# Six units of lag for the downs and three for the gate products, with tile 1's projection in a bank of its own

## The reference

```python
xw = einsum('ntd,dh->nth', x, Wx) + b
def step(prev_h, xw_t):
    next_h = tanh(xw_t + prev_h @ Wh)          # 32 steps, one after another
xf  = hs                                        # what follows is per token
xn  = xf * rsqrt(mean(xf * xf) + EPS) * norm_scale
logits = xn @ wg + bg
vals, idx = top_k(logits, 4);  gates = softmax(vals)
gate_full = einsum('tke,tk->te', one_hot(idx, 16), gates)
h = einsum('th,ehd->etd', xn, w1) + b1
a = minimum(h[..., ::2], 7.0);  b = clip(h[..., 1::2], -7.0, 7.0)
s = a * sigmoid(1.702 * a) * (b + 1.0)
y = einsum('eti,eih->eth', s, w2) + b2
out = x + hs + einsum('eth,te->th', y, gate_full)
```

## Time and profile before

| | us |
|---|---|
| three timed runs, median (lowest, highest) | 108.16 (108.02, 108.65) |
| the profiled execution, its own time | 107.47 |
| span of its trace | 105.7 |
| TensorE busy | 98.3 (93% of the span) |
| VectorE busy | 67.2 (64%) |
| GpSimd busy | 64.7 (61%) |
| ScalarE busy | 61.7 (58%) |

### The profile page before, as it was taken

One profiled execution on the slowest core, in us unless ns is written; L12 is line 12 of the kernel. 1 busy time (PEld: TensorE's weight loads), 2 busy tenths in 40 slices (PEclk: granted clock), 3 DMA queues, 4 the chain that ended last, 5 costly groups with the idle time before them and its releaser, 6 DMA issues.

```text
span 105.7 us, 1704 instructions
## 1 busy us (share of the span) xinstructions
PE 98.3 (93%) x549; PEld 83.6 (79%) x549; DVE 67.2 (64%) x179; ACT 61.7 (58%) x143; POOL 64.7 (61%) x77
## 2 busy tenths in 40 slices
PE   7778899989999999999999979999999999999980
PEld 2557789978999999999999958888777777777660
DVE  0302357976827996589787997668566556666740
ACT  3354836999755586667736646666555666655400
POOL 6004447997890995639963799689544566544400
PEclk9999999999999999999999999999999999999999
DMA  2999920007930000895048911995100000000003
GB/s 66 224 378 338 374 92 0 0 9 254 398 147 3 0 6 6 212 372 212 5 141 228 366 67 20 274 364 207 34 6 0 3 0 0 0 0 0 0 0 99
DMA packets 5000, 12.97 MB, mean 123 GB/s; under 512 B 752, under 2 KB 1792, under 8 KB 4992
## 3 DMA queue, kind: packets, MB, share of 16 engines
q1 hardware_dynamic: 4672, 12.69, 35.5%
q10 hardware_dynamic: 320, 0.18, 0.6%
HBM read 12.28 MB, written 0.59 MB: 122 GB/s over the span
## 4 chain that ended last, share of the span: by engine, by line
PE 82%; ACT 7%; DMA 2%; DVE 2%; POOL 2%; issue 2%; POOLq 0%; DVEq 0%; ACTq 0%
PE psA L806 20%; PE psB L806 19%; PE psY L836 12%; PE psR L836 7%; PE psR L753 5%; PE psY L753 3%; PE psM L836 3%; PE psR L848 2%; DMA wx_x_sb<-in_wx_x 2%; PE psR L745 2%; PE psM L760 2%; ACT small_h L450 2%; ACT psA L494 2%; PE psM L767 1%; ACT psA L503 1%
## 5 line engine op out<-in xcount | busy, mean ns | idle before, releaser
L414 POOL TENSOR_TENSOR actg<-act,gate_cols 128x512 f32<-128x512 f32 x31 | 39.4, 1281 | 12.5 <-DVE act L713 10.7
L696 DVE TENSOR_SCALAR lin<-psB,one_b1b 128x256 f32<-128x256 f32 (+1 forms) x48 | 26.0, 568 | 18.8 <-PE psB L806 18.8
L494 ACT ACTIVATE psA<-psA,lim_b1a 128x256 f32<-128x256 f32 (+1 forms) x48 | 23.8, 513 | 23.2 <-PE psA L806 23.1
L713 DVE SCALAR_TENSOR_TENSOR act<-lin,psA 128x512 f32<-128x512 f32 x32 | 22.0, 686 | 1.8 <-ACT psA L503 0.6
L503 ACT ACTIVATE psA<-psA,limit_col 128x512 f32<-128x512 f32 x32 | 21.1, 659 | 0.8
L806 PE MATMUL psA<-xn_hi,w_hi 128*128 128x256 f32 (+1 forms) x48 | 18.9, 394 | 0.2
L836 PE MATMUL psY<-actg,w_sb 128*128 128x256 f32 x64 | 17.2, 391 | 0.8 <-POOL actg L414 0.8
L806 PE MATMUL psB<-xn_hi,w_hi 128*128 128x256 f32 (+1 forms) x48 | 16.0, 333 | 0.0
L806 PE MATMUL psB<-xn_lo,w_hi 128*128 128x256 f32 (+1 forms) x48 | 15.6, 324 | 0.0
L806 PE MATMUL psB<-xn_hi,w_lo 128*128 128x256 f32 (+1 forms) x48 | 15.5, 323 | 0.0
L806 PE MATMUL psA<-xn_hi,w_lo 128*128 128x256 f32 (+1 forms) x48 | 15.5, 323 | 0.0
(11 more groups left out here) (87 smaller groups left out, 133.7 us busy)
## 6 DMA issues: line engine op xcount, KB each, us to landing
gate_cols<-gate_rows SPq DMA_DIRECT2D x16, 512.0 KB, 5.7
w_sb<-in_w SPq DMA_DIRECT2D x4, 512.0 KB, 7.3
w_sb<-in_w SPq DMA_DIRECT2D x4, 256.0 KB, 8.3
wx_x_sb<-in_wx_x SPq DMA_DIRECT2D x1, 320.0 KB, 5.9
wx_x_sb<-in_wx_x SPq DMA_DIRECT2D x2, 128.0 KB, 2.7
out<-yT SPq DMA_DIRECT2D x2, 128.0 KB, 4.3
out<-yT SPq DMA_DIRECT2D x1, 192.0 KB, 1.9
small_h<-in_small ACTq DMA_DIRECT2D x1, 105.0 KB, 2.8
```

What stands on the lines that cost most here:

```text
L414: nc.gpsimd.tensor_tensor(by_pair(actg[:, u % SUM_DEPTH, w]), by_pair(act[:, u % ACT_DEPTH, w]), gate_block(u, w), ALU.mult).then_inc(actg ...
L494: last = nc.scalar.activation(psA[u % 2][:, o], psA[u % 2][:, o], ACT.Relu, scale=-1.0, bias=lim_b1a[:, e0 + k:e0 + k + 1])
L696: last = nc.vector.tensor_scalar(lin[:, v % 2, o], psB[v % 2][:, o], one_b1b[:, e0 + k:e0 + k + 1], LIMIT + 1.0, ALU.add, ALU.min)
L713: nc.vector.scalar_tensor_tensor(act[:, v % ACT_DEPTH, 0:w], lin[:, v % 2, 0:w], 1.0 - LIMIT, psA[v % 2][:, 0:w], ALU.max, ALU.mult).then_ ...
```

## The change

`LAG` goes from 4 to 6, `POOL_LAG` from 2 to 3, and the rings grow to 8 and 6 buffers. Since add_h(c) stands in slot UNIT0[c + 1] + LAG, it moves from slot 12 to slot 14 for chunk 0, and from 20 to 22 for chunk 1. In the head, tile 1 is projected into `psX`, its sums go to `psX` too (with semaphores of their own), and tiles 2 to 6 are projected one by one in the head; only tile 7's projection is left in the loop, in slot 10 (before: tiles 5 to 7 at once, in slot 6). Both tiles' raw logits are made together behind the sums of tile 1. ScalarE makes all high parts of w1 ahead of slot 0 (before: six of the 16 calls in slots 0 to 2). The gates of pair 0 are transposed between a(1) and b(1), and copied ahead of Gelu(1). GpSimd's gate product stands ahead of the exponentials of its slot. The scaling of the gates becomes two instructions with a scalar operand.

```diff
-    LAG = 4
-    POOL_LAG = 2
-    ACT_DEPTH, SUM_DEPTH = 6, 5
+    LAG = 6
+    POOL_LAG = 3
+    ACT_DEPTH, SUM_DEPTH = 8, 6
...
-    W1_AHEAD, W1_SHARED = 5, 3
-    XW_AT = [0, 0, 1, 1, 2, 1, 2, 3]
-    XW_LATE = 5
+    W1_SHARED = 3
+    XW_AT = [0, 3, 0, 1, 2, 1, 2, 3]
+    XW_LATE = 7
...
-            return (psY if j in (0, 2) else psR)[:, k * P:(k + n) * P]
+            return (psX if j == 1 else psY if j in (0, 3, 4) else psR)[:, k * P:(k + n) * P]
...
-            order = [(k, g) for g in range(last_group(0) + 1) for k in ("stats", "rstd")]
+            order = [("stats", 0), ("rstd", 0), ("rstd", 1)]
...
-                pool.wait_ge(m_read, psM_turn(("stats", g)))
+                if g == 1:
+                    pool.wait_ge(mean_ready, 1)
+                else:
+                    pool.wait_ge(m_read, psM_turn(("stats", g)))
...
+                if v >= POOL_LAG:
+                    gate_product(v - POOL_LAG)
                 for q in at(RSTD, v):
                     power_expo(q)
                     place_expo(q)
-                if v >= POOL_LAG:
-                    gate_product(v - POOL_LAG)
...
-            for k in range(HEAD - W1_AT - 2, 2 * W1_AHEAD):
+            for k in range(HEAD - W1_AT - 2, 2 * NP):
                 w1_high(k)
...
+                if u < LAG:
+                    for q in at(GATES_T, u):
+                        copy_gates(q)
                 acte.wait_ge(relu_done, u + 1)
...
-                if u + W1_AHEAD < NP:
-                    w1_high(2 * (u + W1_AHEAD))
-                    w1_high(2 * (u + W1_AHEAD) + 1)
...
-                nc.vector.tensor_tensor(
-                    gates_w[:, ts, :].rearrange("p j (a b e) -> p j a b e", a=3, b=2)[:, :, :, 0, :],
...
+                for j in pair_tiles(q):
+                    last = nc.vector.tensor_scalar(
+                        gates_w[:, j, :].rearrange("p (a b e) -> p a b e", a=3, b=2)[:, :, 0, :],
+                        gate_sum[:, j, :].rearrange("p (a e) -> p a e", a=1).to_broadcast([P, 3, E]),
+                        inv[:, j:j + 1], None, ALU.mult)
...
                 pe.wait_ge(sq_ready, g + 1)
-                turn(("stats", g))
+                if g != 1:
+                    turn(("stats", g))
...
-                if t == 3:
-                    x_wx(1, 1)
+                if t in (1, 2):
+                    x_wx(t, 1)
+                elif t == TL:
+                    x_wx(3, 1)
                 elif t == TL + 1:
                     pe.wait_ge(consts_ready, 1)
                     sums(0).then_inc(m_mm, 1)
                 elif t == TL + 2:
-                    pe.wait_ge(wg_ready, 1)
-                    raw_logits(range(0, 1), psB[0])
+                    x_wx(4, 1, start=False)
                 elif t == HEAD - 1:
                     lay_rstd(0)
-                    x_wx(2, 1)
-            sums(1).then_inc(m_mm, 1)
-            raw_logits(range(1, 2), psB[0]).then_inc(raw_mm, 1)
-            pe.wait_ge(step_done, HEAD)
-            x_wx(3, 1)
+            x_wx(5, 1, start=False)
+            sums(1).then_inc(sum1_mm, 1)
+            pe.wait_ge(wg_ready, 1)
+            raw_logits(range(0, 2), psB[0]).then_inc(raw_mm, 1)
             lay_rstd(1)
-            x_wx(4, 1, start=False)
+            x_wx(6, 1, start=False)
...
                     for t in steps_at(v, 0):
                         step(t)
+                    for q in at(GATES_T, v):
+                        transpose_gates(q)
...
-                if v < LAG:
-                    for q in at(GATES_T, v):
-                        transpose_gates(q)
```

More of the change, by code:

```diff
@@ L162, in adaln_rnn_moe_kernel @@
         m_mm = sem("m_mm")
+        sum1_mm = sem("sum1_mm")
         raw_mm = sem("raw_mm")
@@ L168, in adaln_rnn_moe_kernel @@
         sq_ready = sem("sq_ready")
+        mean_ready = sem("mean_ready")
         xh_ready = sem("xh_ready")
@@ L506, in _ @@
                     tanh(t)
-                for q in at(GATES_T, u):
-                    copy_gates(q)
+                if u >= LAG:
+                    for q in at(GATES_T, u):
+                        copy_gates(q)
                 for q in at(STATS, u + 1):
                     square(pair_group(q))
-                if u + W1_AHEAD < NP:
-                    w1_high(2 * (u + W1_AHEAD))
-                    w1_high(2 * (u + W1_AHEAD) + 1)
             acte.wait_ge(yT_ready, NC + 1)
@@ L530, in stats @@
                 n = len(ts)
-                dve.wait_ge(m_mm, psM_turn(("stats", g)))
-                mean = nc.vector.tensor_scalar(meansq[:, ts.start:ts.stop], psM[:, 0:n], 1.0 / H, EPS, ALU.mult,
-                                               ALU.add)
+                if g == 1:
+                    dve.wait_ge(sum1_mm, 1)
+                else:
+                    dve.wait_ge(m_mm, psM_turn(("stats", g)))
+                mean = nc.vector.tensor_scalar(meansq[:, ts.start:ts.stop], (psX if g == 1 else psM)[:, 0:n], 1.0 / H, EPS,
+                                               ALU.mult, ALU.add)
                 if g < CHUNKS[0]:
-                    mean.then_inc(m_read, 1)
+                    mean.then_inc(mean_ready if g else m_read, 1)
                 else:
@@ L618, in gates_scale @@
                 settled()
-                ts = slice(2 * q, 2 * q + 2)
-                nc.vector.tensor_tensor(
-                    gates_w[:, ts, :].rearrange("p j (a b e) -> p j a b e", a=3, b=2)[:, :, :, 0, :],
-                    gate_sum[:, ts, :].rearrange("p j (a e) -> p j a e", a=1).to_broadcast([P, 2, 3, E]),
-                    inv[:, ts].rearrange("p (j a e) -> p j a e", a=1, e=1).to_broadcast([P, 2, 3, E]),
-                    ALU.mult).then_inc(scale_done, 1)
+                for j in pair_tiles(q):
[3 more added lines that the diff above has]
+                        inv[:, j:j + 1], None, ALU.mult)
+                last.then_inc(scale_done, 1)
             def gates_low(q):
@@ L751, in step @@
                 if t == TL * XW_LATE:
-                    x_wx(XW_LATE, NT - XW_LATE)
+                    x_wx(XW_LATE, NT - XW_LATE, start=False)
                 nc.tensor.matmul(step_psum(t), wh_sb, hT[:, t * N:(t + 1) * N], start=False, stop=True,
@@ L757, in sums @@
                 pe.wait_ge(sq_ready, g + 1)
-                turn(("stats", g))
+                if g != 1:
+                    turn(("stats", g))
+                bank = psX if g == 1 else psM
                 for k, j in enumerate(group_tiles(g)):
-                    last = nc.tensor.matmul(psM[:, k:k + 1], sq[:, j * P:(j + 1) * P], ones[:, :], start=True, stop=True)
+                    last = nc.tensor.matmul(bank[:, k:k + 1], sq[:, j * P:(j + 1) * P], ones[:, :], start=True, stop=True)
                 return last
```

## The result

The changed kernel takes 112.67 us (median of four executions: 112.17, 112.61, 112.73 and a disturbed one of 324) against 108.35 us before on the same chip: a ratio of 1.038, 95% interval 1.033 to 1.044. That is 4.3 us slower, and outside the forecast's range of 106.1 to 108.2. Of the three others the median is 112.61. The profiled execution took 112.73 us in a span of 110.9.

A forecast was written before the change was run, and what follows sets the result against it. The loop was taken to run at TensorE's pace (93% busy). Gains 0.6 + 0.43 + 0.15 less 0.42 gave 0.76, taken as 0.8 us: 107.35 us from the median 108.16, range 106.1 to 108.2.

The forecast's parts named there:

- 0.1 for the shorter gate scaling (a guess; its ends are 0 and 0.2): Slots 0 to 3: the new scaling form of pair 0 lets a(2) start 0.1 us earlier, besides 0.34 from the routing.
- GpSimd and the deeper rings wait for nothing new: Downs and tail: no new waits there; gain 0, with 0.1 us to either side.
- Head: Before the first up: second sums no longer wait 0.36 us for xn, so a(0) starts at 14.77 instead of 15.11.
- rival 4: Head: x of tiles 3 to 7 comes too late and holds the recurrence; 108.5 us with 1.5 us more lateness; chance 0.12.
- Slots 0 to 3: ScalarE is freed of w1 pairs; a(4) starts at 24.75 instead of 25.66, a gain of 0.9 us.
- Slots 4 and 5: Two downs, 2.1 us together, are owed until later; a(6) starts at 29.8, a gain of 0.7 us.
- The wait in slot 14: First down of chunk 1 waits 1.36 us for add_h(0) to free psY, against 0.94 removed in slot 15.
- rival 1: Slot 14: the wait on psY doesn't come or is small; time 106.05 us; chance 0.1.
- rival 3: Early slots: TensorE's clock rises earlier with the denser head, 0.5 us gained; time 106.85 us; chance 0.1.
- gain of 0.6 at a(8): Slots 4 to 7: a(8) starts at 35.75; act(5) 2.7 behind a(5), with 0.3 taken off for ScalarE's standstill.
- 0.43 for the projections: Slot 6: of 0.65 us for three tiles' projection on TensorE only 0.22 remains, in slot 10.
- rival 2: Early slots give nothing, as VectorE sets a(8) or ScalarE's copies in slot 1 cause lateness; 108.0 us; chance 0.22.

The follow-up runs named there:

- e1: The changed kernel with the gate scaling of before, one tensor_tensor for both tiles instead of two tensor_scalar: 108.43 us, ratio 1.002.
- e3: e1 with add_h one slot earlier, ahead of the routing of pair 3: 108.56 us, ratio 1.001.
- e5: e1 with GpSimd's gate product behind the exponentials again, as before: 107.77 us, ratio 0.993.
- e6: e5 with add_h one slot earlier, ahead of the routing: 107.24 us, ratio 0.989.
- e9: The changed kernel with only GpSimd's old order restored, the two tensor_scalar kept: 109.59 us, ratio 1.013.
- e10: The kernel before with GpSimd's gate product ahead of the exponentials as its only change: 108.91 us, ratio 1.006.
- e7: The kernel before with all 16 of ScalarE's w1 calls ahead of slot 0: six executions between 107.6 and 112.7 us, inconclusive.
- e4: The changed kernel with ten extra VectorE scaling instructions on scratch tiles in the head: one execution, 116.65 us.

## Why the prediction was wrong

**The step that failed** is "0.1 for the shorter gate scaling (a guess; its ends are 0 and 0.2)". The sign was wrong and the lower end excluded what happened. Alone, two of 252 ns replace one of 257, so even without a neighbour the term is a loss of 0.25. In place it was pair by pair 1.49, 2.22, 2.25 and 2.04 us against 1.5 for all four in the old form, and the median rose by 4.24. The term was also applied to pair 0 only, though the edit runs four times.

**A second step failed beside it**: "GpSimd and the deeper rings wait for nothing new". That is true of what GpSimd waits for, and leaves out what it holds up. The product that starts freshly beside the scaling cost 0.66 us with the old form and 3.08 with the new. The forecast gave this move no term of its own.

The row that bears on both was there: of the four old scalings one took 257 ns and three 399 to 419. One operation of one shape with two durations is being held by something. The Trainium skill, page "SBUF — State Buffer", section "Who interferes with whom", has the rule: VectorE and GpSimd share a pair of ports, `tensor_scalar` in a two-port mode or any VectorE instruction with two inputs in SBUF meets a GpSimd instruction that reads SBUF on it, and "whoever issues first gets the shared pair for the whole instruction; the other fully blocks". The traces agree: alone 252 and 257 ns; beside GpSimd each scaling of pairs 1 to 3 ended within about 0.1 us of the end of a GpSimd instruction, in both forms. Whether this `tensor_scalar` ran in a two-port mode no run here shows.

**Right, with a size measured.**

- *Head*: 14.77 forecast. The kernels with the change's head had 14.69 to 14.99 in five profiled executions (e1, e3, e5, e6, e9). The changed kernel's own had 15.28; there a w1 call on ScalarE stood 0.89 us for its weights' DMA, with a tanh of the recurrence behind it:

```profile
7.75 0.42 ACT L463 ACTIVATE w_hi<-w_sb 128x256 fp32r<-128x256 f32 x1 [0.89 <-DMA w_sb<-in_w]
...
12.64 3.77 ACT L463 ACTIVATE w_hi<-w_sb 128x256 fp32r<-128x256 f32 x12
```

  The twelve calls end at 16.4, against 16.0 forecast. The x of tiles 3 to 7 held nothing (rival 4).
- *Slots 0 to 3*, read from e1: a(2) 20.45 (20.35 forecast), b(2) 21.92 (21.8), a(3) 22.86 (22.75), a(4) 25.11 (24.75).
- *Slots 4 and 5*: a(6) 30.07 in e5 (29.8). The place was right and the gain of 0.7 was not: the forecast reckoned it from a chain row, 32.62, and the timeline has a(6) of before at 32.38, which is 30.3 without the two downs. The gain is 0.2.
- *The wait in slot 14*: 1.13 in place of 1.36, released by yT L666 in front of L839, as named; rival 1 falls. In e5 the same wait is 1.1.
- *The clock*: rival 3 falls. In the changed kernel the matmuls of a(1) still start 0.21 us apart (the six go from 18.69 to 19.90); in before they start 0.12 apart (18.44 to 19.12).
- *Slot 15 and the tail*: no down waits for a gate product; behind the last up the two kernels owe six and four downs, as counted.

**Mis-sized**: the gain of 0.6 at a(8), and with it the 0.43 for the projections. In e5, where the scaling of slot 6 is short, a(8) started at 36.58 and not 35.75. VectorE's timeline of e5, then TensorE's of before:

```profile
31.14 0.69 DVE L722 SCALAR_TENSOR_TENSOR act<-lin,psA 128x512 f32<-128x512 f32 x1 [0.39 <-DVE lin L705]
...
35.76 0.67 DVE L722 SCALAR_TENSOR_TENSOR act<-lin,psA 128x512 f32<-128x512 f32 x1
```

```profile
29.47 0.37 PE L806 MATMUL psA<-xn_hi,w_hi 128*128 128x256 f32 x1
...
38.72 0.36 PE L806 MATMUL psA<-xn_hi,w_hi 128*128 128x256 f32 x1
```

From the start of act(5) to the end of act(6) are 5.29 us, as carried over (5.24), and a(8) follows act(6) by 0.15, as forecast. What was late is the start of act(5): a(5) started at 27.96 (27.65 forecast), and act(5) 3.18 behind it, not 2.7. Before, it was 3.21 behind a(5)'s 29.47, so the change brought almost nothing here: 0.2 of the difference comes from counting 3.0 from the chain's 29.64, and the 0.3 taken off for ScalarE's pause wasn't there. So the mechanism of rival 2, VectorE setting a(8), did hold, and cost the 0.83. In the trace e5 then has no lead over before: 38.72 less 36.58 is 2.14, which is the two downs that it still owes. That holds although the projection of 0.65 us is gone from slot 6: where VectorE sets a(8), less work on TensorE ahead of it gains nothing. Both end their last down at 102.7.

The sum was too high by its own places, too. Its a(8) at 35.75 is a lead of 0.83 on before (38.72 less the two downs), and that lead has the projection of slot 6 in it; with 0.22 paid back in slot 10, 0.61 are left for the two terms that the sum has as 0.6 + 0.43.

**And yet e5 is 0.7% faster by the executions that were timed.** The profiled execution of before lay 0.7 below its median at the time of the forecast and 0.9 to 1.1 below those of these sessions; e5's lay 0.27 below its own. So against the traces the forecast's gain of 0.76 measured 0.0, and against the medians the change without its two scaling faults (e5) measured 0.6 to 0.7. No trace of a usual execution of before was taken, but one of e10 was, which is the kernel before up to slot 4. Its timeline of TensorE:

```profile
18.66 0.56 PE L806 MATMUL psA<-xn_hi,w_hi 128*128 128x256 f32 x1
...
21.74 0.37 PE L806 MATMUL psA<-xn_hi,w_hi 128*128 128x256 f32 x1
```

There a(1), the first row, still ran with its matmuls 0.21 us apart, and the pace doubled only inside b(1), at about 20.9; in the profiled execution of before it had doubled ahead of a(1). So a(2), the second row, started 6.48 behind a(0) (15.26) and not 5.65: 0.83 later. The forecast was worked out from an execution with the early rise. How often it comes early is not known, and that this is the whole of the 0.9 to 1.1 is not shown; the exposed first down that e7 shows is another candidate.

**The account.** From 112.67: old form, 4.24 less (e1, 108.43); old order of GpSimd, 0.66 less (e5, 107.77); add_h ahead of the routing, 0.53 less (e6, 107.24). The forecast of 107.35 is 0.42 below e5, the kernel that has all else of the change.

## What to carry to other kernels

Before changing the form or place of a small VectorE instruction, list what GpSimd has in flight beside it. Beside the products and subtractions here (256 and 512 columns) its price was the remainder of the GpSimd instruction, and each of the two instructions that replaced one paid it anew. Two durations of one shape in the trace of before are a sign. Equally, moving a GpSimd instruction is a change to VectorE: its cost is to be read from what VectorE runs at the new time, not from what GpSimd waits for. And where a profiled execution is 0.6% below its median, gains of that size can't be read from it step by step.

## What the runs showed of the hardware that wasn't expected

- The hold is not on all pairs. VectorE's `hot` (two inputs in SBUF) ran 0.29 us at 60.71 in the changed kernel, inside GpSimd's exponential on 6 columns. So did all 16 of before, after, e1 and e5, each inside an exponential and each 291 to 295 ns. By the rule quoted above it should have been held; the trace shows that it wasn't, and why is open.

```profile
60.71 0.29 DVE L610 TENSOR_TENSOR hot<-iota_e,top_f 128x128 f32<-128x128 f32 x1
60.92 0.41 DVE L666 TENSOR_TENSOR yT<-wx_x_sb,psY 128x256 f32<-128x256 f32 x1
...
61.76 0.45 DVE L564 CAST xn_hi<-xn 128x256 fp32r<-128x256 f32 x1
```

```profile
60.26 1.32 POOL L381 TENSOR_TENSOR expo<-euler,diff 128x6 f32<-128x6 f32 x1 [0.75 <-DVE diff L597]
61.66 0.41 POOL L389 TENSOR_TENSOR hot<-hot,expo 128x128 f32<-128x128 f32 x1
```

- A cast is held too: the one at 61.76 took 0.45 us beside a GpSimd multiply that ended at 62.07; in e5, at 33.87, beside the end of the exponential (32.69 to 34.01), it took 0.29.
- A stall of TensorE can cost more than its length. In e7 the granted clock fell to 0.50, the 1.2 GHz level, during the wait of 2.37 and stayed there past 35 us; in e4 it fell to 0.50 about 1 us behind a wait of 1.69 that ended at 38.23, for some 10 us. The changed kernel's wait of 1.68 at 38.61 went by with the clock full, so the length of the wait alone doesn't decide it.
- Pair 0 in slot 1 doesn't fit the simple picture in the old form. With GpSimd's w1 subtractions beside it, the `tensor_tensor` took 257 to 260 ns (before, e1, e5), while the first `tensor_scalar` alone took 0.80 and the pair 1.49. The phase is the same to 0.01 us: the scaling starts 0.66 behind the first subtraction in e5 and 0.67 in e9. So here the form decides and not the place; why is open. VectorE's and GpSimd's timelines of e5, then those of e9:

```profile
18.46 0.26 DVE L629 TENSOR_TENSOR gates_w<-gate_sum,inv 128x96 f32<-128x96 f32 x1
```

```profile
17.80 2.91 POOL L402 TENSOR_TENSOR w_lo<-w_sb,w_hi 128x256 fp32r<-128x256 f32 x4
```

```profile
18.44 1.48 DVE L629 TENSOR_SCALAR gates_w<-gate_sum,inv 128x48 f32<-128x48 f32 x2
```

```profile
17.77 2.78 POOL L402 TENSOR_TENSOR w_lo<-w_sb,w_hi 128x256 fp32r<-128x256 f32 x4
```
